# Attention projections on one core: one instruction for the product with swapped halves, and the first roundings of the attention on ScalarE

## The reference, cut to what matters

```
q = einsum('bsd,ed->bse', x, Wq).reshape(bsz, seqlen, 32, 128)    # k: 8 heads
q = rmsnorm(q, q_norm_w); k = rmsnorm(k, k_norm_w)                # over the 128 of a head
t1, t2 = t[..., :64], t[..., 64:]
rope(t) = concatenate([t1 * cos - t2 * sin, t2 * cos + t1 * sin])
```

## Time and profile before

| | us |
|---|---|
| median of three runs | 2469.86 (2467.91 to 2471.93) |
| the profiled execution | 2471.95 |
| its span, first to last instruction | 2470.4 |
| PE busy | 2403.2 (97%) |
| DVE busy | 1785.0 (72%) |
| ACT busy | 1602.7 (65%) |

### The profile page before, as it was taken

How to read it: one execution, slowest core, us unless ns; L and a number is a source line. 1 busy time by engine, 2 the same in 40 slices (tenths; PEclk the granted TensorE clock), 3 DMA queues, 4 the chain that set the end, 5 groups by cost and what they waited for, 6 DMA issues and landing times.

```text
span 2470.4 us, 54824 instructions
## 1 busy us (share of the span) xinstructions
PE 2403.2 (97%) x16070; PEld 2184.4 (88%) x16071; DVE 1785.0 (72%) x3674; ACT 1602.7 (65%) x3335; POOL 610.5 (25%) x896
## 2 busy tenths in 40 slices
PE   6899899999999989999999999999999999899999
PEld 4688788888888779999999999999999999688887
DVE  5454429999898978888788888878888887644443
ACT  3243337777787778888888888888888888311111
POOL 1200040000000034544444444444444443000000
PEclk9899999999999989999999999999999999999999
DMA  6622332333333388998898899888888987766663
GB/s 218 190 81 69 114 123 82 109 103 99 98 118 109 104 262 298 293 302 288 291 296 298 285 296 301 287 294 296 297 284 295 304 285 250 270 229 220 212 206 139
DMA packets 377209, 536.84 MB, mean 217 GB/s; under 512 B 49698, under 2 KB 263394, under 8 KB 374306
## 3 DMA queue, kind: packets, MB, share of 16 engines
q1 hardware_dynamic: 304994, 311.62, 39.7%
q0 software_dynamic: 70016, 221.30, 26.2%
q10 hardware_dynamic: 2112, 2.89, 0.4%
HBM read 437.35 MB, written 98.30 MB: 217 GB/s over the span
## 4 chain that ended last, share of the span: by engine, by line
PE 61%; DVE 1%; DMA 1%; ACT 1%; issue 0%; SPq 0%; DVEq 0%; ACTq 0%
PE both_ps_o L1709 18%; PE both_ps_s L105 10%; PE both_ps_s L103 10%; PE both_ps_s L104 9%; PE both_ps_pt L1686 9%; PE both_ps_o L1712 5%; DMA out_w_stage<-in_wo 1%; PE both_ps_s L1692 1%; DVE out_w_lo L1885 0%; DMA out_inv<-inv_t 0%; PE both_ps_s L1694 0%; DMA k_own<-qkv_out_t 0%; DVE out_o L1956 0%; DVE out_o_lo L1960 0%; DVE att_prob L1424 0%
## 5 line engine op out<-in xcount | busy, mean ns | idle before, releaser
L1709 PE MATMUL both_ps_o<-att_pt,att_v 128*128 128x128 f32 x4096 | 540.2, 275 | 0.0
L1406 ACT ACTIVATE att_prob<-att_prob,att_shift 128x544 f32<-128x544 f32 x512 | 384.4, 751 | 203.0 <-DVE att_shift L1424 188.6
L1709 PEld LDWEIGHTS both_ps_o<-att_pt,att_v 128*128 128x128 f32 x4096 | 504.8, 191 | 0.0
L1424 DVE CUSTOM_DVE_ANT_0 att_prob<-both_ps_s,att_mask 128x544 f32<-128x544 f32 x512 | 364.9, 713 | 0.0
L1401 DVE TENSOR_TENSOR att_k_lo<-att_k_raw,att_k_hi 128x1024 fp32r<-128x1024 f32 (+1 forms) x320 | 338.5, 1058 | 1.9 <-ACT att_k_hi L1389 1.9
L103 PE MATMUL both_ps_s<-att_k_hi,att_q_hi 128*128 128x272 f32 x1024 | 338.5, 331 | 0.6 <-DVE att_k_lo L1401 0.5
L1686 PE MATMUL both_ps_pt<-both_ident,att_prob 128*128 128x128 f32 x2048 | 308.6, 273 | 3.1 <-ACT att_pt L1580 3.1
L105 PE MATMUL both_ps_s<-att_k_hi,att_q_lo 128*128 128x272 f32 x1024 | 297.1, 290 | 0.0
L1580 ACT ACTIVATE att_pt<-both_ps_pt 128x512 f32<-128x512 f32 x512 | 294.7, 576 | 0.9 <-PE both_ps_pt L1686 0.7
L104 PE MATMUL both_ps_s<-att_k_lo,att_q_hi 128*128 128x272 f32 x1024 | 294.4, 288 | 0.0
L1389 ACT ACTIVATE att_k_hi<-att_k_raw 128x1024 fp32r<-128x1024 f32 x315 | 287.9, 914 | 0.0
(11 more groups left out here) (217 smaller groups left out, 5032.5 us busy)
## 6 DMA issues: line engine op xcount, KB each, us to landing
att_k_raw<-in_k_pages SPq DMA_DIRECT2D x1024, 128.0 KB
q_t<-qkv_out_t SPq DMA_DIRECT2D x128, 256.0 KB
att_q_raw<-q_t POOLq DMA_DIRECT2D x64, 512.0 KB
o_t<-att_o POOLq DMA_DIRECT2D x64, 512.0 KB, 7.0
out_inv<-inv_t SPq DMA_DIRECT2D x32, 1024.0 KB, 7.0
out_o<-o_t SPq DMA_DIRECT2D x32, 1024.0 KB, 6.9
both_w_stage<-in_w_qkv SPq DMA_DIRECT2D x12, 1024.0 KB, 5.1
l_w_stage<-in_w SPq DMA_DIRECT2D x8, 1024.0 KB, 7.6
```

The source lines that it names most:

```text
L1406: act.activation(prob[:, b, :], prob[:, b, :], ACT.Exp, bias=shift[:, b:b + 1], scale=-1.0, accum_out=total[:, j // HK, j % HK:j % HK + 1] ...
L1424: dve.tensor_tensor_reduce(out=prob[:, b, :].rearrange("p (a n) -> p a n", a=2), in0=ps_s[:, j % 2, :, 0:HALF], in1=mask[:, j // HK, :].re ...
L1709: pe.matmul(out, v_sb[p][:, c, h * DH:(h + 1) * DH], pt_sb[:, j % OG, c, :], start=(c == 0), stop=False)
```

## The change

The two instructions of `cross_part`, each on 128x256, become one on 128x512: its input `normed` is read with the two halves of each head in reverse order. It stands where the first of the two stood, ahead of the reciprocal; nothing stands in the place of the second, between `same_part` and the sum. The semaphore `b_ready` is counted once per step. The six roundings of `HI_AHEAD` leave DVE, where they stood after the reciprocal of their step, and go to the end of the same step's list on ACT (`hi_part` for sequence 0).

```diff
-        def cross_part(n, j, which, half):
+        def cross_part(n, j, which):
             p, t = j % 2, j % NT
             dve.wait_ge(normed_ready, n + 1)
             dve.tensor_tensor(
-                part_b[:, p, :, half * H:(half + 1) * H], normed[:, p, :, (1 - half) * H:(2 - half) * H],
-                cross[which][:, t:t + 1, half * H:(half + 1) * H].to_broadcast([P, 4, H]), ALU.mult).then_inc(b_ready, 1)
+                part_b[:, p, :, :].rearrange("p g (a d) -> p g a d", a=2),
+                normed[:, p, :, :].rearrange("p g (a d) -> p g a d", a=2)[:, :, ::-1, :],
+                cross[which][:, t:t + 1, :].rearrange("p t (a d) -> p t a d", a=2).to_broadcast([P, 4, 2, H]),
+                ALU.mult).then_inc(b_ready, 1)
...
             dve.wait_ge(a_ready, n + 1)
-            dve.wait_ge(b_ready, 2 * n + 2)
+            dve.wait_ge(b_ready, n + 1)
...
                 if is_step(b, j, 2):
-                    cross_part(*step_before(b, j, 2), 0)
+                    cross_part(*step_before(b, j, 2))
...
                     same_part(*step_before(b, j, 2))
-                    cross_part(*step_before(b, j, 2), 1)
                     rotate(*step_before(b, j, 2))
...
-    def first_hi_part(dve, c):
-
-        raw, hi, _ = piece(c, 0)
-        dve.wait_ge(k_loaded[0][c], 16 * (1 if c == PIECE_Q else pages_of(c)[1]))
-        dve.tensor_copy(hi, raw).then_inc(hi_done, 1)
-
...
     def scalar_ahead(act, j):
 
+        if j in HI_AHEAD:
+            hi_part(act, 0, 1, 0, HI_AHEAD[j])
         if j == STEPS + 1:
             exponential(act, 0, 0)
...
-        if j in HI_AHEAD:
-            first_hi_part(dve, HI_AHEAD[j])
```

## The result

| | before | changed |
|---|---|---|
| median of 10 runs each | 2470.06 (2466.0 to 2474.5) | 2475.35 (2473.42 to 2480.01) |
| ratio, 95% interval | | 1.0023 (1.0015 to 1.0032) |
| the profiled execution, its span | 2471.95, 2470.4 | 2474.37, 2472.9 |

The changed kernel is slower by 5.3 us; the forecast was 5.0.

What follows compares the result with a forecast made beforehand. PE bounds blocks 1 to 4, the ACT-DVE loop the last block; the merged product lengthens the loop. Terms +5.8, -0.85, -0.34, +0.35 sum to +5.0 us on 2469.86: 2474.9, range 2470.5 to 2480.0.

Steps and rivals of the forecast that it cites:

- What bounds: Projections: PE bounds blocks 1 to 4 at 3.193 us a step; the ACT-DVE loop, 2.93 us a turn, decides.
- The slot, 0.60: Merged product between sum and reciprocal takes 0.60 us of DVE's list, making that part 1.20 where it was 1.05.
- Rival (1): Merged product's slot is 0.58, not 0.60: +2.0 us, 2471.9; chance of 0.57 to 0.59: 0.17.
- rival (3): Merged product's reverse read costs: at a slot of 1.12, 76 us more, 2551; chance 0.12, anything above 0.63 included.
- Rival (2): Merged product fits under ACT's root, slot 0.45 or less, loop stays at 2.93: -3.5 us, 2466.3; chance 0.09.
- Blocks 1 to 4, +5.8: From block 1 to step 3 of the last block, 129 longer turns, 32 with a `w_lo`, add 5.8 us.
- PE's lead: Blocks 1 to 4: DVE and ACT may be some 4.7 us late before a transpose waits; lateness carries on.
- Rival (4): Blocks 1 to 4's 1.0 us per block is never called in: 2468.7; chance counted within rival (1).
- The last block, -0.85: Steps 4 to 24, bound by the loop before and after: shorter and longer turns together change by -0.85 us.
- The end, -0.34: From the reciprocal of step 24 to the last transposes: 18.94 us where it was 19.28, -0.34.
- The tail, +0.35: After the multiplies, SP's store waits for pages and a copy-out: between 0 and 0.7 us added, 0.35 taken.
- The attention, unchanged: The attention stage starts later by the whole delay and is as long as before.

Runs made afterwards that it cites:

- e4: Changed kernel with ACT's squares of a step put ahead of the normalising of the step before: 2462.59 us, 0.9966 of before.
- e6: Kernel before, its two half products kept as two instructions but both issued ahead of the reciprocal: 2485.79 us, 1.0062 of before.
- e5: Changed kernel with the merged product reading `normed` forward, halves not swapped: 2473.2 us (one run).
- e10: Changed kernel with the merged product over three of the four heads, 128x384 in place of 128x512: 2460.04 us (one run).
- e1: Changed kernel with the six roundings back on DVE, so the merged product alone: 2475.97 us, 1.0018 of before.
- e8: e4 with DVE's work on the lengths and row numbers two steps later in the last block: 2461.77 us, 0.9960 of before.
- e11: Changed kernel with e4's order on ACT and the roundings back on DVE: 2463.12 us, 0.9968 of before.
- e7: Kernel before with only e4's reordering of ACT, halves and DVE's roundings left as they were: 2469.68 us, 0.9996 of before.

## Why the prediction was right, and where its terms were off

- **What bounds.** Right. The argument was that time taken off DVE's list is worth nothing in blocks 1 to 4 and that a loop through both engines decides; e4 cuts the loop and the loss is gone, e6 has the loss without the merge.
- **The slot, 0.60.** Measured 0.60, in every turn in which the reciprocal doesn't wait. Rival (1), 0.58, and rival (3), the price of a reversed read, are out (e5). The Trainium skill (Vector Engine (DVE) Microarchitecture Reference, Measured stream behaviour on trn2) gave an estimated 0.608 for a forward read; the mean slot of 150 turns is 0.600. The trace agrees with it to about 1%, for the negative step too, which the page has no measurement of.
- **Rival (2), the product under the root.** e10 bears out its sum, -3.5, with -3.46 in the stretch, and the cover of 0.45, past which its slot of 0.467 adds 0.02 to the way from sum to reciprocal. No run has a slot between 0.335 and 0.467. The whole product is 0.15 too long for the cover.
- **Blocks 1 to 4, +5.8.** Measured, from the first transposes to the reciprocal of step 3 of the last block: 789.26 - 377.77 = 411.49 against 784.14 - 379.40 = 404.74, **+6.75**. The turns themselves were 3.073 and 3.673, for which the sum was 0.3 too high. What was missed are two turns at the ends of blocks 2 and 3, of 3.71 and 3.58 where 3.07 was due: +1.15 (below). That is the mis-sized term.
- **PE's lead.** PE's steps grew beyond 3.193 from step 5 of block 3 on (3.29 there, up to 3.46 in the block, 3.39 to 3.42 in block 4). Rival (4) is out; that the loop's lateness would be called in by then was said.
- **The last block, -0.85.** Measured 75.22 against 76.39, **-1.17**. Plain turns (+0.14 each, 4 of them), step 12 (+0.27) and step 9 (-0.44) came as worked out. The steps with extra work ahead of `same_part` shed 0.24 and not 0.19 each, since `rotated` starts 0.72 and not 0.75 after `same_part`, and the reciprocal 1.19 after the sum. Steps 11, 13, 16 and 19 took 3.49, +0.19 together for the 0.1.
- **The end, -0.34.** Measured 883.47 - 864.48 = 18.99 against 19.28, **-0.29**. Multiplies end +5.29 for the +4.65 forecast.
- **The tail, +0.35 taken of 0 to 0.7.** Measured 895.32 - 883.47 = 11.85 against 11.23, **+0.62**: near the upper end. To there the whole is 5.9, 0.9 more than the forecast; the 5.3 of the medians lies between, and the scatter of the runs doesn't tell them apart.
- **The attention, unchanged.** From that copy-out to the first multiply of the output projection 1211.74 before and 1209.59 after. Of the 13 traces nine have 1209.6 to 1209.8 and four (before, e1, e8, e11) 1211.0 to 1211.7, and kernels with and without the merge are in both groups. So these 2 us don't follow the change; where they come from was not followed up. They and the 1.6 ahead of the changed code are why the two profiled executions lie only 2.4 apart.

The forecast of +5.0 was right for its reason. Up to the end of the tail the sum was 0.9 too small, nearly all of it the two turns at the ends of blocks 2 and 3; that the medians come within 0.3 of it is closer than the sum deserved.

## What to carry to other kernels

Before taking work out of an engine's list, ask which closed path through the engines is longest, and on which side of each hand-over the work lies: here up to 0.24 us per step came out of DVE's list and 0.15 went into the loop, and the kernel paid for the 0.15. A cover, such as the 0.45 us of a root on another engine, has an edge: up to it work is free, beyond it every step pays, and one instruction in place of two can't be split across it. When an edit that shortens the work makes a kernel slower, look for the order that makes the bound the list instead of the loop; one swap of two items in ACT's list turned the same edit from 5 us lost to 7 us gained.

## What the runs showed that was not expected

**ACT starts late where a program loop jumps back.** Timeline of DVE, then of ACT, in the changed kernel at the end of block 2:

```profile
571.40 0.69 DVE L1165 TENSOR_REDUCE qkv_sumsq<-qkv_squares 128x4 f32<-128x512 f32 x1 [0.40 <-ACT qkv_squares L1048]
...
573.24 0.18 DVE L1161 RECIPROCAL qkv_inv_rms<-qkv_rms 128x4 f32<-128x4 f32 x1 [0.55 <-ACT qkv_rms L1054]
```

```profile
569.05 0.30 ACT L1054 ACTIVATE qkv_rms<-qkv_sumsq,qkv_eps 128x4 f32<-128x4 f32 x1 [0.27 <-DVE qkv_sumsq L1165]
...
572.91 0.30 ACT L1054 ACTIVATE qkv_rms<-qkv_sumsq,qkv_eps 128x4 f32<-128x4 f32 x1 [1.05 <-DVE qkv_sumsq L1165]
```

The sum is over at 572.09, and the root starts 0.82 later, where a turn earlier it started 0.03 after the sum's end. The profile names the sum as what ended the wait, but the sum had long been done. It happens at the ends of blocks 2 and 3 and not at those of 1 and 4. Blocks 2, 3 and 4 are the three passes of the program's loop (`chunk_pairs`, line 951) and the others are written out, so the two places are the two jumps back to the start of the loop; entering it and leaving it show nothing. In the kernel before, the same place reads:

```profile
571.11 0.30 ACT L1054 ACTIVATE qkv_rms<-qkv_sumsq,qkv_eps 128x4 f32<-128x4 f32 x1 [1.82 <-issue]
```

It was there to be read, an idle time of ACT of 1.8 us that no other engine had caused, and PE's lead covered it. Once the loop of ACT and DVE binds, it is paid: 0.64 and 0.51 in the changed kernel, 0.40 and 0.33 in e6. That its cause is the jump itself and not, say, the loading of the instructions behind it is not shown; no run here took the program's loop away.

**A short instruction behind the one it needs.** A half of 0.335 right ahead of `rotated` kept it waiting to 0.51 (e7), while the merged order has 0.12 of such a gap behind `same_part` (0.70 for 0.58). Of the 0.24 us per step that merging takes from DVE's list, 0.07 is the instruction saved. The gap ahead of `rotated` gives 0.175 less the 0.12, and the wait for the root, 0.115 in e7, gives the rest.
